# A two-layer graph kernel: low part behind the sieves, products between high and low halves, result rows normalised on GpSimd

## The reference, cut to what matters

```
h = relu(layernorm(x));  x = x + (A @ (h @ W + b)) / deg          # first layer, 3327 rows, 256 columns
h = relu(layernorm(x));  X = Xf = Xb = Xa = h                     # second layer
Rf = S / rowsum(S);  Rb = S / colsum(S)                           # S = adj + I
for s in range(2):                                                # "first step", "second step"
    logits = (Xa @ W1) @ W2 @ (Xa @ W3).T                         # 3327 x 3327
    keep, per row, the largest logits until their softmax mass reaches 0.9
    A = softmax over the kept logits
    Xf, Xb, Xa = Rf @ Xf, Rb @ Xb, A @ Xa
    Z += Xf @ U1[s] + Xb @ U2[s] + Xa @ U3[s]
x = x + layernorm(X + Z) * gamma + beta
```

## Time and profile before

| | us |
|---|---|
| median of 3 runs | 2000.2 (1999.85 to 2000.92) |
| profiled execution, device time | 1999.62 |
| its span, first to last instruction | 1997.6 |
| busy in the span: PE, DVE, ACT, POOL | 1777.0, 1634.1, 1364.9, 605.1 |
| first high part of the first step (L937) | starts at 342.40 |
| first pass of the second step (L1502) | starts at 1090.96 |

### The profile page before, as it was taken

The page is one execution under the profiler, slowest core; times in us unless marked ns, Lnnn a source line. Parts: engine busy times, 40 slices in busy tenths (PEclk is TensorE's granted clock), DMA queues, the critical chain, the costliest instruction groups (busy, mean ns, idle before and its releaser), DMA issues.

```text
span 1997.6 us, 37487 instructions
## 1 busy us (share of the span) xinstructions
PE 1777.0 (89%) x11660; PEld 1312.2 (66%) x11660; DVE 1634.1 (82%) x3964; ACT 1364.9 (68%) x2201; POOL 605.1 (30%) x1056
## 2 busy tenths in 40 slices
PE   4999964899999999993976699999999999999997
PEld 3888832677777777773763466666666676767665
DVE  5444467899999999998864899999999999999987
ACT  5222266888888888983835568686868686777752
POOL 4000131244444444441341132324242323232330
PEclk9999976899999999997988899999999999999998
DMA  6999721454444444442433010101010101010122
GB/s 170 196 202 203 195 100 56 97 117 117 112 105 116 106 111 114 110 108 56 112 77 125 22 42 21 42 21 42 21 42 21 42 21 42 21 41 22 38 91 72
DMA packets 235345, 168.26 MB, mean 84 GB/s; under 512 B 188451, under 2 KB 220577, under 8 KB 235168
## 3 DMA queue, kind: packets, MB, share of 16 engines
q1 hardware_dynamic: 221264, 117.44, 21.6%
q0 software_dynamic: 3744, 22.14, 7.2%
q10 hardware_dynamic: 10288, 28.12, 4.2%
HBM read 107.99 MB, written 37.49 MB: 73 GB/s over the span
## 4 chain that ended last, share of the span: by engine, by line
issue 35%; DVE 21%; PE 19%; POOLq 9%; DVEq 7%; POOL 4%; DMA 2%; ACT 2%; ACTq 0%
DVE probs_t L1588 7%; DVE stats L1595 5%; POOLq L720 5%; PE lg L1165 2%; DMA probs_t<-row_scalars 2%; PE bank L1096 2%; PE bank L1095 2%; PE bank L1079 2%; PE lg L1096 2%; PE lg L1095 2%; PE bank L1200 2%; DVEq L1783 1%; DVE sorted_e L1614 1%; PE bank L1052 1%; DVEq L1612 1%
## 5 line engine op out<-in xcount | busy, mean ns | idle before, releaser
L1188 PE MATMUL bank<-both,s_tile 128*128 128x512 f16 x1352 | 302.4, 381 | 16.9 <-issue 16.9
L1257 PE MATMUL bank<-xcur,probs_t 128*128 128x256 f32 x1352 | 296.1, 379 | 0.0
L1165 PE MATMUL lg<-k_t,q_tile 64*128 64x512 f32 (+1 forms) x820 | 191.6, 568 | 96.1 <-DVE expo L1485 89.1
L1257 PEld LDWEIGHTS bank<-xcur,probs_t 128*128 128x128 f32 x1352 | 255.0, 190 | 33.6
L1188 PEld LDWEIGHTS bank<-both,s_tile 128*128 128x128 bf16 x1352 | 132.8, 98 | 166.7 <-issue 20.0
L1485 DVE TENSOR_SCALAR_CACHE_REDUCE expo<-lg 128x1024 f32 (+1 forms) x208 | 206.8, 1023 | 43.1 <-PE lg L1165 27.4
L660 POOL TENSOR_TENSOR window<-window,probs_t 128x832 f16<-128x832 f32 x104 | 215.2, 2069 | 81.1 <-ACT probs_t L937 68.6
L1165 PEld LDWEIGHTS lg<-k_t,q_tile 64*128 64x128 f32 x820 | 69.3, 192 | 178.6 <-DVE expo L1485 123.1
L868 ACT ACTIVATE expo<-expo,below_max 128x3327 f32<-128x3327 f32 x52 | 159.4, 3065 | 24.7 <-DVE below_max L1493 23.7
L699 POOL TENSOR_TENSOR aims<-found 128x2 f32<-128x2 f32 x26 | 5.1, 195 | 555.6 <-ACT found L903 555.6
L1588 DVE SCALAR_TENSOR_TENSOR probs_t<-expo,mine 128x1664 f32 (+3 forms) x54 | 156.4, 2896 | 8.4 <-issue 8.0
(11 more groups left out here) (303 smaller groups left out, 3628.6 us busy)
## 6 DMA issues: line engine op xcount, KB each, us to landing
s_tile<-s_scratch SPq DMA_DIRECT2D x28, 832.0 KB, 4.5
expo<-in_adj POOLq DMA_DIRECT2D x25, 831.8 KB, 9.7
s_tile<-s_scratch ACTq DMA_DIRECT2D x24, 832.0 KB, 4.5
s_scratch<-s_tile SPq DMA_DIRECT2D x14, 832.0 KB, 10.1
s_scratch<-probs_t SPq DMA_DIRECT2D x6, 832.0 KB, 9.3
s_scratch<-window SPq DMA_DIRECT2D x6, 832.0 KB, 9.6
q_tile<-q_scratch SPq DMA_DIRECT2D x104, 32.0 KB, 2.1
xa_scratch<-ht ACTq DMA_DIRECT2D x26, 128.0 KB, 2.2
```

The costliest lines, as they stand in the source:

```text
L1165: last = T.matmul(lg[c % 2][:, h * CHUNK:h * CHUNK + w], q_tile[b][DA * h:DA * (h + 1), :], k_all[DA * h:DA * (h + 1), s, c0:c0 + w], star ...
L1188: last = T.matmul(s_ps[:, 0:width], s_tile[b][:, k, :], moving, start=(k == 0 and part == 0), stop=(k == NT - 1 and part == 1))
L1257: last = T.matmul(kept_ps[1][:, 0:D], probs_t[:, k * P:(k + 1) * P], xcur[:, k, :], start=(k == 0), stop=(k == NT - 1))
```

## The change

- First step, GpSimd: the second chunk of the low part waits for the first sieve of the next tile, the third chunk for its second sieve (the fourth follows it).
- First step, DVE: `take_above` writes the second half first, after the low part has been made (its transposed copy need only be complete before the first half); the row maximum's offset is a tensor_scalar.
- First step, PE: the 52 matmuls of the high part of the next tile are placed ahead of this tile's products with U; those of the low part come behind the turned rows, with the late logits after 18 of the 26 blocks.
- Second step: DVE only reduces the maxima (L1493 goes) and does so behind the copy of `lead`; ACT derives the two offsets by two activations on one column. `first_bracket` is cut in two: nine instructions and the first point can run after the first refinement, the second point and the rest (15) after the second. y_in is added on GpSimd (`add_result`), and ACT takes the moments one tile later; GpSimd normalises the whole row (`normalise_result`).
- End: DVE only adds the first layer's result, in five pieces, each written out at once; in the last tile, the turned rows and part of the products run ahead.

```
@@ probs_low (GpSimd)
+                    if c in (1, 2) and not is_last(t):
+                        pool.wait_ge(sieves, t * 2 + c + 2)
                     last = G.tensor_tensor(natural_lo[:, cols], window[:, cols], natural_hi[:, cols], ALU.subtract)
@@ results of the second step (GpSimd)
-            def centre_result(t, m, b):
+            def add_result(t, m, b):
+                y = tile3(y_all, tile_of(m, b))
+                pool.wait_ge(y_out[1], t + 2)
+                pool.wait_ge(y_loaded[1], DMA * (t + 1))
+                G.tensor_tensor(y, y, y_in[:, :], ALU.add).then_inc(y_added, 1)
+            def normalise_result(t, m, b):
                 pool.wait_ge(y_moments, t + 1)
-                G.tensor_tensor(y, y, mean[:, bass.ds(tile_of(m, b), 1)].broadcast_to([P, D]), ALU.add)
+                G.tensor_tensor(y, y, mean[:, column].broadcast_to([P, D]), ALU.add)
+                G.tensor_tensor(rstd[:, column], var[:, column], share, ALU.mult)
+                G.tensor_tensor(rstd[:, column], rstd[:, column], least_var, ALU.add)
+                G.tensor_tensor(rstd[:, column], rstd[:, column], minus_half, ALU.pow)
+                G.tensor_tensor(y, y, rstd[:, column].broadcast_to([P, D]), ALU.mult)
-                G.tensor_tensor(y, y, gamma_sb, ALU.mult).then_inc(y_centred, 1)
+                G.tensor_tensor(y, y, gamma_sb, ALU.mult)
+                G.tensor_tensor(y, y, beta_sb, ALU.add).then_inc(y_centred, 1)
...
+                if not (isinstance(t, int) and t >= NT - 2):
+                    first_bracket(t + 2, m + 1, b)
+                if not (isinstance(t, int) and t == 0):
+                    normalise_result(t - 1, m - 1 + b, 1 - b)
+                if not is_last(t):
+                    add_result(t, m, b)
@@ exponentials (ScalarE, second step)
+                    if s == 1:
+                        for j in range(2):
+                            A.activation(below_max_all[:, b, j:j + 1], tops[:, b:b + 1], ACT.Identity, scale=-1.0, bias=offsets[:, j:j + 1])
@@ step (ScalarE, second step)
+                    if before is not None and not is_last(t):
+                        act.wait_ge(y_added, t + 1)
                     if more:
                         refine(b, 1)
+                    if before is not None and not is_last(t):
+                        added_result(*before)
@@ first_step (TensorE)
-                    attend(t)
-                    if left(3):
-                        logits(t + 3, 1 - b, m + 2 + b, LOGITS_LATE)
                     turn_diffused()
+                    attend(t, 1, (t + 3, 1 - b, m + 2 + b, LOGITS_LATE) if left(3) else None)
...
                     query_key(b)
+                    if left(1):
+                        attend(t + 1, 0)
                     products(t, False)
@@ last_result (TensorE, last tile)
+                    product(0, xfbt[:, 0:DC, :])
+                    turn_kept(t, b)
+                    T.matmul(lg[0][:, 0:D], ident[:, :], y_in[:, :], start=False, stop=False, skip_group_check=True)
+                    product(1, xfbt[:, DC:2 * DC, :])
+                    pe.wait_ge(x_t_ready[1], t + 1)
+                    product(2, xt).then_inc(y_done[1], 1)
@@ step (VectorE)
-                        dve.wait_ge(lo_turned, t * DMA + DMA)
-                        take_above(b, False, 0, N // 2)
+                        dve.wait_ge(lo_made, t + 1)
+                        take_above(b, False, N // 2, N)
...
+                    if s == 0:
+                        dve.wait_ge(lo_turned, t * DMA + DMA)
+                    take_above(b, s == 1, 0, N if s == 1 else N // 2)
```

More of the change, by code:

```diff
@@ L53 @@
 KEPT_AT = (10, 20)
+LOGITS_AT = 18
 LATE_AFTER = (1, 3)
@@ L720, in first_bracket @@
                     pool.drain()
+                pool.wait_ge(first_counted, t + 1)
+                G.tensor_tensor(minus_slack, ends_t[:, 0:1], found[:, b, 6:7], ALU.subtract)
+                G.tensor_copy(lead[:, b, 4:7], found[:, b, 4:7])
+                G.tensor_scalar(ends, ends_t[:, :], whole, None, ALU.mult)
+                pool.drain()
+                G.tensor_tensor(ends, ends, ends_c[:, :], ALU.add)
+                offer(0)
+                pool.wait_ge(expo_ready[1], t + 1)
+                offer(1)
                 G.tensor_tensor(span[:, :], lead[:, b, 10:12], lead[:, b, 8:10], ALU.subtract)
@@ L1190, in diffuse, with attend @@
                     last.then_inc(s_done[s], 1)
-                def attend(t):
-                    pe.wait_ge(xa_ready[0], t + 2)
-                    for p, (turned_p, ready) in enumerate(((turned_hi, hi_turned), (turned_lo, lo_turned))):
-                        if is_last(t):
-                            next_logits(((0, 1), (2,))[p])
-                        pe.wait_ge(ready, t * DMA + 2 * DMA)
-                        for k in range(NT):
-                            for part in range(2):
-                                last = T.matmul(kept_ps[0][:, 0:D], turned_p[:, k, :], parts[:, k, part * D:(part + 1) * D],
-                                                start=(p == 0 and k == 0 and part == 0),
-                                                stop=(p == 1 and k == NT - 1 and part == 1))
-                    last.then_inc(pv_done[0], 1)
+                def attend(t, p, late=None):
+                    if p == 0:
+                        pe.wait_ge(xa_ready[0], t + 2)
+                    turned_p, ready = ((turned_hi, hi_turned), (turned_lo, lo_turned))[p]
+                    if is_last(t):
+                        next_logits(((0, 1), (2,))[p])
+                    pe.wait_ge(ready, t * DMA + 2 * DMA)
+                    for k in range(NT):
+                        if late is not None and k == LOGITS_AT:
+                            logits(*late)
+                        for part in range(2):
+                            last = T.matmul(kept_ps[0][:, 0:D], turned_p[:, k, :], parts[:, k, part * D:(part + 1) * D],
+                                            start=(p == 0 and k == 0 and part == 0), stop=(p == 1 and k == NT - 1 and part == 1),
+                                            skip_group_check=True)
+                    if p == 1:
+                        last.then_inc(pv_done[0], 1)
                 def turn_diffused():
@@ L1705, in step @@
                     if s == 0:
+                        if not is_last(t):
+                            highest(other)
                         dve.wait_ge(cut_ready, t + 1)
@@ L1711, in step @@
                         V.tensor_copy(mine[:, :], lead_of(b))
-                        dve.drain()
+                        if is_last(t):
+                            dve.drain()
+                        else:
+                            highest(other)
                         evaluate(b)
                         dve.wait_ge(p_flipped, t * NG + 1)
-                    rank(b)
+                    rank(b, s == 0)
                     flag(s == 1).then_inc(flags_ready[s], 1)
@@ L1806, in _ @@
                 copy_logits(0, 0, [NL - 1] if s == 1 else LOGITS_EARLY + LOGITS_LATE)
+                highest(0)
+                dve.drain()
                 copy_logits(1, 1, LOGITS_EARLY)
@@ L1813, in _ @@
                                     accum_out=lower_count).then_inc(counted, 1)
-                if s == 1:
+                if s == 0:
+                    for b in range(2):
+                        dve.wait_ge(team_stored[b], DMA * stores_of(NTEAM + (NTEAM + b) % 2))
+                else:
                     dve.wait_ge(lo_turned, DMA * (NT + 1))
```

182 lines of the change are left out of this document (108 added, 74 removed).

## The result

The changed kernel takes 2003.65 us (median of 20 runs, 2000.32 to 2007.58) against 2000.31 for the kernel before (20 runs): a ratio of 1.0015, 95% interval 1.0009 to 1.0022. So it is slower by 0.15%, a small loss that is clear of the noise. The forecast was 1985, between 1970 and 1999. The profiled execution took 2002.59 us, its span is 2000.9; that of the kernel before was 1997.6, so 3.3 us have to be found.

What follows compares the result with a forecast made beforehand. ScalarE was taken to bound the first step (25.8 us per tile), VectorE the second; -14.2 (first step) + 5 - 2.6 - 1.5 - 1.7 = -15.0 us took 1999.6 to 1984.6, or 1985 beside the median, range 1970 to 1999.

Steps and rivals of the forecast that it cites:

- Does the later low part hold anyone?: First step: low part ready at 17.5 us, TensorE there at 19.0, so 1.5 us of cover and no wait.
- VectorE's stalls: First step: sieve stalls of 1.45 and 0.82 us go, L1493's too; a new one of 1.3 us comes at L1597.
- ScalarE sets the pace: First step: ScalarE needs 25.8 us per tile, VectorE then 24.7; 16 tiles by 0.15 us give -2.4 us.
- Tiles 0 to 5, -7.3: Start of the first step: first tile 25.7 us, four at 25.8, so 128.9 us against 136.2.
- Repairs, -5.5: First step, three tiles where VectorE ranks once more because flags ask for it: 114.5 us against 120.0.
- Last tile, +1: First step's last tile: TensorE is the bound, high-half products wait ahead of the last low part, +1 us.
- Start of the second step, -2.6: VectorE waits 6.60 us for the bracket's 24 instructions; nine now run earlier, so -2.6 us.
- Steady tiles of the second step: VectorE saves 0.28 us, loses 0.5 meeting GpSimd per tile: net +0.22 by 23 tiles, +5 us (-6 to +26).
- The last tile's bracket, -1.5: Second step's last tile: VectorE's 3.31 us wait for its bracket shortens, GpSimd's wide instructions meet what follows: -1.5 us.
- The very end, -1.7: Behind the last L1014: only the last two of six products remain there, the first ones run earlier: -1.7 us.
- The gates give nothing: TensorE waits for the low part: Rival, first step: TensorE waits for the late low part, tile stays at 25.96 us, total 1999; chance 0.13.
- Slower by GpSimd's meetings: Rival, second step: L1711, L1502 and L1516 wait in every tile, net 1.1 by 23 = +26 us, total 2006; chance 0.10.

Runs made afterwards that it cites:

- e2_s_behind: The changed kernel with the load of s_tile issued by SyncE behind the low part's transposition and the flags, instead of by ScalarE: 1986.09 us, ratio 0.9933.
- e6_scalar_longer: e2_s_behind with one 128x512 copy more on ScalarE in each first-step tile: 26.35 us per tile; one run, 1994.84 us.
- e9_s_behind_no_gates: e3_old_first_step with the load of s_tile issued by SyncE behind the low part and the flags: 1988.24 us, ratio 0.9939.
- e5_s_behind_old_order: e2_s_behind with TensorE's order of the first step put back as before the change: 1983.97 us, ratio 0.9918.
- e3_old_first_step: The changed kernel without gates and with TensorE's and VectorE's old first-step orders; second step and end as changed: 1991.38 us, ratio 0.9958.
- e4_before_early_load: The kernel before, with ScalarE issuing the load of s_tile some 7 us earlier, beside the low part's transposition: one run, 1996.77 us.
- e8_collision_old_order: The changed kernel, gates and s_tile's load unchanged, with TensorE's order of the first step as before: 2063.61 us, ratio 1.0342.
- e10_collision_logits_first: e8_collision_old_order with the late logits put between the high and the low half instead of behind the low half: 2044.65 us, ratio 1.0218.

## Why the prediction was wrong

**The step that failed** is the one under "Does the later low part hold anyone?": 8.9 for the second sieve, 3.8 for two chunks, "and the transpose's 4.8 us make 17.5", against 19.0 for TensorE, "so 1.5 us of cover". Measured from 690.71: the sieve ends at 10.1, the chunks at 13.9, the part lands at 22.2, and TensorE is there at 20.4. TensorE came 1.4 us later than I had counted and the sieve 1.2, which nearly cancel; the transfer took 8.2 us (median) instead of 4.8, and the cover of 1.5 us became a wait of 1.8. That term was mis-sized, because I took its duration from where it stood before, alone on the queues, and did not ask what stands where it goes: the load of s_tile, which ScalarE starts 0.2 us after the transposition has landed in the kernel before, and which was in the trace. With 4.8 us there the cover is what was forecast (e2_s_behind: 703.5 against 702.1, 1.4 us).

**Point by point.**
- VectorE's stalls: right. Sieves at 1.95 us, the new stall at 1.1 instead of 1.3. A second one, L1709 at 0.8 us, was missed: it comes with VectorE running earlier against GpSimd's next instruction.
- "The flags lose nothing": wrong. SyncE issues them in time, but the transfer takes 3.0 us instead of 1.9 beside the load, and VectorE waits 1.2 us.
- "ScalarE sets the pace", 25.8 us per tile: right once nothing collides (25.86 and 25.82; e6_scalar_longer). But that the 0.15 us per tile would come from the gates is not borne out: moving the load alone takes the tile from 25.97 to 25.82 (e9_s_behind_no_gates), and the gates add nothing to that. What ScalarE saves by it, one transfer less to issue or something else, is not shown.
- Tiles 0 to 5, -7.3: too much even without the collision; e5_s_behind_old_order has 133.1 us there against 136.2, -3.1. The first tile is right (25.7, measured 25.68), but ScalarE still waits for VectorE twice in the second tile (2.3 and 3.0 us).
- Repairs, -5.5: e5 has K from tile 21 to 25 in 141.85 us against 144.11, -2.3.
- Last tile, +1: it was +2.3, by TensorE's new order. Start of the second step, -2.6: near. From TensorE's turned rows of the last tile to the next K it is 56.74 us in the kernel before, 54.28 in e3_old_first_step and 54.5 in e5 and e9; the wait ahead of the copy of `lead` falls from 6.60 to 4.56 in e3.
- Steady tiles of the second step: -0.28 us right, stalls of 0.5 too much. VectorE at the start of two tiles in a row:

```profile
1573.32 0.39 DVE L1804 COPY mine<-lead 128x16 f32 x1
...
1574.00 3.76 DVE L1591 SCALAR_TENSOR_TENSOR scraps<-expo,mine 128x3327 uint8 x1
...
1606.86 0.17 DVE L1804 COPY mine<-lead 128x16 f32 x1
...
1607.32 3.71 DVE L1591 SCALAR_TENSOR_TENSOR scraps<-expo,mine 128x3327 uint8 x1
```

GpSimd is busy until K + 5.4 in the first of these tiles, where K + 5.9 was counted, but only the copy is held, by 0.2 us in this tile and up to 0.4 in others, and the pass by under 0.1; the rest of the time it is GpSimd that is held. Its last addition, beside those two rows:

```profile
1573.64 0.64 POOL L755 TENSOR_TENSOR parts<-parts,y_tile 128x256 f32 x1
...
1607.51 4.02 POOL L755 TENSOR_TENSOR parts<-parts,y_tile 128x256 f32 x1
```

So VectorE's stalls are 0.0 to 0.4 us, and the net is -0.17 us per tile.
- The last tile's bracket, -1.5: VectorE's wait did fall from 3.31 to 1.11 us, but GpSimd's row results then meet seven of its small instructions and it is given back to the hundredth. One of them in VectorE's timeline:

```profile
1960.15 0.73 DVE L1709 TENSOR_SCALAR scraps<-prefix,mine 128x40 f32<-128x40 f32 x1
```

And the GpSimd instruction it met:

```profile
1960.11 0.72 POOL L769 TENSOR_TENSOR parts<-parts,k_t 128x256 f32<-128x256 f32 x1
```

- The very end, -1.7: it was -2.9. From the end of the weighted sum to the result row's move it is 3.3 us instead of 5.3; the rest is gained in the transposes of kept values ahead of it.

**The rivals.** "The gates give nothing: TensorE waits for the low part" had a chance of 0.13 and was the right mechanism; but the gates did not merely give nothing, they cost 8.6 us, since the wait is added to every tile. I had read "for: the transpose moves behind two sieves", and weighed it by the cover alone. "Slower by GpSimd's meetings" did not come: those of the second step are the small ones above. Its threshold was also wrong in itself: the other terms of the forecast add up to -20.0 us, which stalls of 0.28 + 20.0 / 23 = 1.15 us per tile would eat, and not 0.9. Of the signs named beforehand, "TensorE idle ahead of the low part's first matmul" is the one that shows.

**A number that looks right by luck.** e2_s_behind, the changed kernel without the collision, takes 1986.1 us, 1 us from the forecast. Its parts are not those of the forecast: up to the K of tile 25 it gains 6.8 us where 15.2 were counted, and the 23 steady tiles of the second step gain 4.4 us where a loss of 5 was counted. The two errors cancel.

## What to carry to other kernels

A step that is moved brings its transfers along: lay the new interval over every other queue's transfers before taking a duration from the old place, since here moving the one transfer that overlapped was worth 17.6 us. Where a gate makes A wait for B, follow the results of A round to B: if they come back, a wait on the way is paid in every turn, and it can grow (from 26.5 to 29.3 us per tile, of which a lower clock on the engine that waits can be up to a third). And to see whether a stalled engine sets the pace, lengthen it by an instruction, as was done with ScalarE; but put the instruction where the engine is not held anyway, or, as with VectorE here, the stall swallows it and the run tells nothing.

## What the runs showed of the hardware

- Two transfers that overlapped slowed each other: the transposition of 128x3328 fp16 takes 4.8 us alone and 8.2 when an 832 KB load starts 2.0 us after it, while the load takes 6.0 instead of 4.5. The pair is done about 8.2 us after the first was issued, little less than the 9.3 of one behind the other. With the load first by 2.1 us (e4_before_early_load) it is 6.9 and 5.7, so the transposition pays the larger part in both orders. A transfer of 0.5 KB issued beside them takes 3.0 us instead of 1.9.
- The exclusion of VectorE and GpSimd also held GpSimd: its addition, started 0.19 us behind VectorE's pass of 3.71 us (1607.32), takes 4.02 us instead of 0.64 and ends 0.50 us behind that pass. In the tile before it starts 0.36 us ahead of the pass (1573.64), takes its 0.64 us, and the pass 3.76 instead of 3.69: tenths of a us decided between these two tiles which engine paid. On VectorE it held not only two-input instructions, but also a copy (`lead`, 0.39 instead of 0.17 us, over at 1573.71, GpSimd's L771 at 1573.68) and a tensor_scalar (L1709, 1.06 instead of 0.24 us, over at 708.57, GpSimd's L664 at 708.53).
- Behind an idle time of 3.4 us TensorE's granted clock fell to 0.50 of full speed for some 3 us in e8_collision_old_order, and 52 matmuls took 7.57 us instead of 5.92; behind other waits of 3.07 to 3.72 us it stayed at 1.00, as it did behind the 1.78 us of the changed kernel's tile from 690.71. In e10_collision_logits_first it was at 0.50 from 713 to 719 us, behind an idle time that ended after 5.35 us.
